# The hats of all fourteen columns formed by ScalarE in SBUF, and every engine's order drawn up anew

## The reference, cut to what matters

```python
out = relu(bn(conv1x1(x)))
offset = conv3x3(out)                      # 18 rows: (dy, dx) for each of 9 taps
py = y + k // 3 - 1 + dy;  px = x + k % 3 - 1 + dx
val = bilinear samples of out at (py, px), zero outside
out = relu(bn(conv1x1(bn(einsum("bckhw,ock->bohw", val, w)))))
```

## Time and profile before

| | us |
|---|---|
| median of 3 runs | 1134.95 |
| lowest and highest | 1133.67, 1144.43 |
| the profiled execution | 1137.99 |
| its span, first to last instruction | 1135.9 |
| busy in it: PE, DVE, ACT, POOL | 949.5, 766.0, 552.7, 355.2 |
| TensorE clock granted, mean share | 0.87 |
| moved by DMA | 123.31 MB |

### The profile page before, as it was taken

How to read it: one execution, slowest core, us unless ns; L and a number is a source line. 1 busy time by engine, 2 the same in 40 slices (tenths; PEclk the granted TensorE clock), 3 DMA queues, 4 the chain that set the end, 5 groups by cost and what they waited for, 6 DMA issues and landing times.

```text
span 1135.9 us, 19270 instructions
## 1 busy us (share of the span) xinstructions
PE 949.5 (84%) x7176; PEld 651.0 (57%) x7176; DVE 766.0 (67%) x2047; ACT 552.7 (49%) x1155; POOL 355.2 (31%) x320
## 2 busy tenths in 40 slices
PE   3779798998889898989889898989898998867534
PEld 2546476665656565756566665656575665545222
DVE  2658375868778795959596876968595958555232
ACT  1134353737365564647383736546464737261502
POOL 2012415243233414152433323250515233233100
PEclk9688769899999898989898996979898989886756
DMA  9011251424425161615243442516161524334160
GB/s 221 16 33 29 60 170 41 149 89 119 136 79 179 55 194 52 201 36 173 80 150 101 119 136 75 180 54 194 48 189 50 152 85 131 114 97 143 27 170 15
DMA packets 116546, 123.31 MB, mean 109 GB/s; under 512 B 64802, under 2 KB 99750, under 8 KB 116454
## 3 DMA queue, kind: packets, MB, share of 16 engines
q1 hardware_dynamic: 103492, 83.33, 26.0%
q10 hardware_dynamic: 6818, 25.04, 6.4%
q0 software_dynamic: 6144, 13.71, 4.0%
HBM read 84.32 MB, written 37.73 MB: 107 GB/s over the span
## 4 chain that ended last, share of the span: by engine, by line
PE 52%; DVE 15%; DMA 10%; issue 9%; ACT 6%; POOL 5%; SPq 1%; ACTq 1%; POOLq 0%; DVEq 0%
PE ps L620 49%; DMA y_turned<-b_yt 6%; POOL b_yp L1234 4%; DMA b_yp<-y_turned,b_to 4%; DVE x L1280 2%; ACT c_pad L955 2%; DVE y L1277 1%; PE ps L834 1%; DVE st L1307 1%; SPq L1795 1%; DVE b_adt L1272 1%; ACT y L955 1%; DVE b_yt L1283 1%; DVE y L1280 1%; PE ps L798 1%
## 5 line engine op out<-in xcount | busy, mean ns | idle before, releaser
L1234 POOL DMA_INDIRECT b_yp<-y_turned,b_to x64 | 82.5, 1289 | 311.0 <-DMA y_turned<-b_yt 296.4
L620 PE MATMUL ps<-y,inw 128*128 128x392 f32 x384 | 141.4, 506 | 0.2 <-DVE y L1277 0.2
L1186 POOL TENSOR_TENSOR rs<-ve,root 128x4 f32<-128x4 f32 x64 | 65.8, 1029 | 219.4 <-DVE ve L1276 219.0
L620 PE MATMUL ps<-c_w,c_zt 126*64 126x196 f32 x896 | 109.2, 400 | 21.5 <-DMA c_zt<-z_turned 18.0
L1307 DVE BATCH_NORM_STATS2 st<-x 128x6 f32<-128x196 f32 x256 | 73.5, 349 | 76.8 <-POOL x L1186 68.0
L620 PE MATMUL ps<-w,a_S 128*32 128x384 f32 (+2 forms) x1280 | 91.9, 431 | 26.2 <-DVE a_S L1280 24.1
L620 PEld LDWEIGHTS ps<-c_w,c_zt 126*64 126x64 f32 x896 | 73.7, 168 | 53.7 <-issue 36.4
L1272 DVE TENSOR_TENSOR c_w<-c_w,c_hat 126x1176 f32<-126x1176 f32 (+1 forms) x64 | 97.6, 1580 | 8.9 <-DMA c_w<-hat_turned 8.9
L955 ACT ACTIVATE x<-ps,cvec 128x392 f32<-128x392 f32 x32 | 18.7, 587 | 167.1 <-PE ps L620 167.1
L620 PEld LDWEIGHTS ps<-y,inw 128*128 128x128 f32 x384 | 69.3, 193 | 39.5 <-issue 3.0
L1208 POOL DMA_INDIRECT x_turned<-b_xt,b_to x64 | 63.6, 994 | 55.1 <-DVE b_xt L1283 43.1
(11 more groups left out here) (201 smaller groups left out, 2087.4 us busy)
## 6 DMA issues: line engine op xcount, KB each, us to landing
z_turned<-c_z SPq DMA_DIRECT2D x32, 441.0 KB
c_zt<-z_turned SPq DMA_DIRECT2D x16, 882.0 KB
c_w<-hat_turned ACTq DMA_DIRECT2D x16, 771.8 KB
c_w<-hat_turned SPq DMA_DIRECT2D x16, 771.8 KB
c_w<-hat_turned ACTq DMA_DIRECT2D x16, 578.8 KB
c_w<-hat_turned SPq DMA_DIRECT2D x16, 578.8 KB
b_xp<-x_turned SPq DMA_DIRECT2D x32, 222.0 KB
x<-in_x SPq DMA_DIRECT2D x32, 196.0 KB, 2.7
```

What stands on the lines that cost most here:

```text
L620: return nc.tensor.matmul(o, l, r, start=start, stop=stop)
L1186: return nc.gpsimd.tensor_tensor(out=o, in0=x, in1=y, op=op)
L1234: nc.gpsimd.indirect_dma_start(out=YP[:, m, h].rearrange("p b d -> p (b d)"), out_offset=None, in_=y_dram[g % 2], in_offset=bass.IndirectO ...
```

## The change

The constant `expand` gives, for the column part, the distance without the column: the sampled place px itself, the same on all 14 partitions of a tap. ACT keeps |py - vy| from f2.3 (Abs) and copies px beside it; f2.4 applies Relu to the row half alone. A new step f2.6 of ACT, four parts (two column pieces by two samples), forms the column hats in `c_w`: one Abs per column with bias -vx, 28 per group in all, and then one Relu with scale -1 and bias 1 over the piece. Its first part waits until PE has read the first six columns of the group before (`c_free`), its third until the accumulation before is finished. The stores and loads of hats go, with their semaphores and DRAM tensor, from SP and from ACT. DVE's product waits for `c_near` instead of the load. PE's instructions stay the same, but for the count after d2.2c. All of `PLAN` and `FROM` is new; `FROM` steps by 56793 per group, where it stepped by about 60897.

What follows from the new tables for a middle group (g), as the order in which parts stand:

- PE: n0(g), s1.1d to f(g-2), o1.0a(g-3), c0.8(g-1), o1.0b, k3.3(g-5), ta.0a(g-2), c0.10(g-1), o1.2a, b, ta.0b, c, c0.11, ta.0d, d2.2a, b(g-4), n2(g-3), c0.13(g-1), d2.2c to g(g-4), f2.1(g-3), d2.4(g-4), c0.1(g), n3(g-4), f2.2(g-3), c0.2(g), f2.3, f2.5a to d(g-3), n1(g-1), k3.1(g-4), f2.5e to h, c0.4(g), tb.7, 10, 11, 12(g-2), s1.1a, b(g-1), tb.20(g-2), c0.5(g), k3.2(g-4), tb.21a, b(g-2), s1.1c(g-1), c0.6(g).
- ACT: c0.1(g), f2.1(g-3), tb.0(g-2), k3.0(g-4), f2.3(g-3), tb.3(g-2), f2.4, f2.5a, b, k3.1, f2.5c, d, c0.4(g), tb.9, tb.10(g-2), **f2.6a, b(g-3)**, tb.20(g-2), s1.1a, b(g-1), tb.21(g-2), c0.5(g), **f2.6c**, k3.2(g-4), **f2.6d**, s1.1c, d(g-1), c0.7(g), s1.1e, f, s1.2, s1.4, c0.8(g), c0.10, k3.3a, ta.0a, k3.3b, o1.2(g-2), ...
- SP: x load of g, ta.3(g-3), tb.22(g-3), f2.6(g-4), d2.1(g-4), store of the result (g-6). Before, f2.5, f2.6, d2.0 and d2.1 of g-4 stood ahead of tb.22(g-3).

```diff
-            expand[at + 2, 1, k] = k % 3 - 1 - np.arange(HW)
+            expand[at + 2, 1, k] = k % 3 - 1
...
 # PE, d2.2
+                    if part == 2:
+                        last.then_inc(c_free.sem, 1)
...
 # ACT, f2.3
-                    fn(c_hat[b][:, :, :].rearrange("p x n -> p (x n)"), R.tile(("ex", b), g)[0:TV, 0:2 * N], ACT.Abs)\
-                        .then_inc(R.drained(("ex", b), g), 1)
+                    t = R.tile(("ex", b), g)
+                    fn(c_hat[b][:, 0, :], t[0:TV, 0:N], ACT.Abs)
+                    fn(c_hat[b][:, 1, :], t[0:TV, N:2 * N], ACT.Copy).then_inc(R.drained(("ex", b), g), 1)
 # ACT, f2.4
-                    x = c_hat[b][:, :, :]
+                    x = c_hat[b][:, 0, :]
                     fn(x, x, ACT.Relu, scale=-1.0, bias=1.0).then_inc(c_hat_ok.sem, 1)
...
+                if i == 6:
+                    h, b = part // G, part % G
+                    if part == 0:
+                        if first(g):
+                            act.wait_ge(ranked, 1)
+                        else:
+                            act.wait_ge(c_free.sem, c_free.count(g - 1))
+                    if part == G and g:
+                        filled(act, "acc", g - 1, H)
+                    drained(act, ("ex", b), g)
+                    cols = VSPLIT[h]
+                    for vx in range(cols.start, cols.stop):
+                        last = fn(c_w[b][:, vx, :], c_hat[b][:, 1, :], ACT.Abs, bias=-float(vx))
+                    last.then_inc(c_apart.sem, 1)
+                    act.wait_ge(c_apart.sem, c_apart.count(g, part + 1))
+                    x = c_w[b][:, cols, :]
+                    fn(x, x, ACT.Relu, scale=-1.0, bias=1.0).then_inc(c_near.sem, 1)
...
 # DVE, d2.1
-                    v.wait_ge(*hat_in[b][h].at(g))
+                    v.wait_ge(c_hat_ok.sem, c_hat_ok.count(g, b + 1))
+                    v.wait_ge(c_near.sem, c_near.count(g, part + 1))
...
 # SP, f2.5 gone
-                    sp.wait_ge(c_hat_ok.sem, c_hat_ok.count(g, b + 1))
-                    sp.dma_start(hat_dram[g % 2][b].rearrange("t (v n) -> (t v) n", v=HW), c_hat[b][:, 1, :])\
-                        .then_inc(hat_out[b].sem(g), 16)
 # SP and ACT, d2.0 gone
-                    load_hats(sp, 0, part, g)
-                    load_hats(act, 1, part, g)
```

More of the change, by code:

```diff
@@ L236 @@
-    "once": (84039,),
+    "n0": (0, 56793, 113586, 170379, 227172, 283965, 340758, 397551, 454344, 511137, 567930, 624723, 681516,
+        738309, 795102, 851895),
+    "c0": (0, 56793, 113586, 170379, 227172, 283965, 340758, 397551, 454344, 511137, 567930, 624723, 681516,
+        738309, 795102, 851895),
+    "n1": (0, 56793, 113586, 170379, 227172, 283965, 340758, 397551, 454344, 511137, 567930, 624723, 681516,
+        738309, 795102, 851895),
+    "s1": (0, 56793, 113586, 170379, 227172, 283965, 340758, 397551, 454344, 511137, 567930, 624723, 681516,
+        738309, 795102, 851895),
@@ L237 @@
+    "once": (0,),
 }
@@ L250 @@
-        (297390,),
-        (300106, 300746, 302963),
-        (61968, 106689, 119060),
+        (8985,),
+        (52229, 56876, 59874, 62685, 63959, 64065, 66772, 70906, 80609, 93597),
+        (115294,),
+        (118326, 118806, 120447, 122707, 122707, 122931),
+        (125505, 128858, 133753, 137402),
+        (175000, 175000, 175000, 175000, 175000, 175000, 175000, 175709, 177066, 177066),
+        (179724, 180523, 184493, 185293),
+        (201722,),
+        (211260, 226189, 228832, 228832, 228832, 228832, 228832, 229220, 229456, 229456, 229834),
@@ L253 @@
+        (250989, 256881, 263977, 265303, 265588, 266448, 266448, 270176),
+        (281812,),
+        (285916, 290610, 294110),
+        (64065, 67667, 102457),
     ),
     "vector": (
[L255 to L260, removed]
@@ new lines @@
+        (88148, 95706),
+        (102906, 115992, 122547, 125928),
+        (132258, 134277, 145401),
+        (145401, 152283, 152495, 152495, 152495, 153570, 154420, 159699, 159699, 160584, 160584, 160584, 160584,
+        162774, 165677, 165677, 165677, 171572),
+        (182845, 186630),
+        (189584, 191394, 196270),
+        (202362, 209076, 209076, 210622, 211214),
+        (226587, 226587, 234567, 239468, 257797, 257877),
+        (257877, 258468, 258779),
+        (301783, 312375),
@@ L304 @@
         (),
-        (725433, 726423),
-        (745848, 745848),
-        (),
-        (),
-        (793133, 793133, 794662, 794662),
-        (795338, 799009, 801675),
-        (),
-        (966006,),
-        (545804, 576221),
+        (461002, 462247),
+        (472862, 472862),
+        (),
+        (),
+        (537059, 537935),
+        (537935,),
+        (),
+        (657912,),
+        (266502, 275592),
     ),
@@ L582, in build @@
         z_in = landed("z_in")
-        hat_out = [landed(f"hat_out{b}") for b in range(G)]
-        hat_in = [[landed(f"hat_in{b}_{h}") for h in range(2)] for b in range(G)]
+        c_apart = sig("distances", 2 * G)
+        c_near = sig("hats_along_row", 2 * G)
+        c_free = sig("c_w_read")
         c_w_ok = sig("c_w", 2 * G)
@@ L600, in drained @@
             eng.wait_ge(ring.drained(f, g), ring.done(f, g))
[L602 to L609, removed]
-            lo, hi = VSPLIT[h].start * N, VSPLIT[h].stop * N
-            eng.dma_start(c_w[b][:, VSPLIT[h], :].rearrange("p v n -> p (v n)"),
-                          hat_dram[g % 2][b][:, lo:hi].unsqueeze(1).to_broadcast([TAPS, HW, hi - lo]))\
-                .then_inc(hat_in[b][h].sem(g), 16)
         block = ctx.enter_context(nc.Block())
```

134 lines of the change are left out of this document (51 added, 83 removed), and 6 rows, old and new, of the table PARTS.

## The result

The changed kernel takes 1183.5 us (median of 4, 1180.31 to 1185.31) against 1137.99 us for the kernel before (median of 4, 1133.67 to 1144.43): a ratio of 1.039, 95% interval 1.033 to 1.045. It is slower by 4%, where 1130 us was forecast with a range up to 1176. The profiled execution took 1183.74 us.

What follows compares the result with a forecast made beforehand. TensorE bounds the kernel, through an order in which it also waits. Steps +5, filling +4, draining -11 on 1137.99 us gave 1136, then 1133 at the median, shaded to 1130 us; range 1082 to 1176.

Steps and rivals of the forecast that it cites:

- The queue of SyncE: Sync queue issuing y_turned earlier: up to 3 us off the gather path; stall of 2.40 us falls to 0.5 (0 to 2.5).
- covered by some 5 us: Sync queue: c_zt sets out later, but its store and load land before d2.2a with some 5 us to spare.
- PE's own work does not change: TensorE in the new order: its own work stays as before, so the step changes only by stalls, +0.3 us.
- rival C: ACT becomes the pacer between Exp and b_us: step of 63.8 us, 1168 us; chance 0.27, clock included.
- The hats: Hats on ACT: 28 Abs, 7.8 us, and four Relus, 5.4 us, add 13.2 us per pair of samples.
- `c_pad`'s 2.6 us: TensorE, new order: c_pad must wait for c0.1, leaving PE 2.6 us idle per step, against 1.40 before.
- The ring: Seven PSUM tiles: the sixth z product waits for a tile ACT copies after Ln, some 0.7 us (0 to 1).
- `c_off`, 1.4: TensorE waits for c_off behind other DVE work: 1.4 us per step, against 0.48 before.
- Filling: Start of the kernel: the first pair's last transposes stand behind the second pair's work, +4 us (0 to +6).
- draining: End of the kernel: without the hats' loads ahead of c_zt it is shorter, taken as -11 us.
- Rival B: The new order closes PE's gaps: step of 59 us, 1092 us; chance 0.28.
- the summed stalls, 6.2 us: TensorE's stalls per step after the change: 6.7 us summed, say 6.2 allowing for overlap, against 5.9 before.

Runs made afterwards that it cites:

- e10: Changed kernel, z_turned store and order kept, with the c_zt load (and the result's stores behind it) waiting until the y gather has landed: 1089.18 us, ratio 0.961.
- e12: Changed kernel with the z_turned store moved ahead of y_turned and the c_zt load made to wait for y_turned's landing: 1108.82 us, ratio 0.978.
- e3: Changed kernel without the four Relus of a group on c_w (that part of the computation left out): 1169.41 us, ratio 1.027.
- e9: Changed kernel with the z_turned store moved ahead of y_turned and without the four Relus on c_w: 1079.28 us, ratio 0.954.
- e7: Changed kernel with the z_turned store, behind y_turned on the sync queue, waiting until the y gather has landed: 1160.38 us, ratio 1.018.
- e2: Functions of the kernel before (hats through DRAM) in the changed kernel's order, with the z_turned store ahead of y_turned: 1120.31 us, ratio 0.981.
- e6: Kernel before with an extra unread store of z_turned's size (2 x 441 KB) right behind the y_turned store: 1151.58 us, ratio 1.006.
- e11: Kernel before with an extra unread 882 KB copy, the size of c_zt, started when y_turned has landed: 1173.72 us, ratio 1.038.
- e5: Changed kernel's functions (hats on ACT) in the order of the kernel before, some later parts moved to follow the hats: 1148.92 us, ratio 1.012.

## Why the prediction was wrong

**The step that failed** is in "The queue of SyncE": "up to 3 us come off this path, and the stall of 2.40 us goes ... 0.5 us stays (0 to 2.5)". It measured 0.52 + 4.59 = 5.1 us in the step shown, 77.6 us in all. Two products use the gathers. In the kernel before either of them waits: in the step of the earlier trace rows the second, 2.40 us, in the step of the earlier trace rows the first:

```profile
366.17 0.59 PE L834 MATMUL ps<-c,b_yp 98*128 98x98 f32 x4 [1.32 <-DMA b_yp<-y_turned,b_to]
```

For the first product the forecast came true: from the copy of `b_yt` to it 8.8 us (10.7 in that step before), with 0.52 us of wait, as forecast. The second is the one that failed. I had seen that `z_turned` and `c_zt` now go out behind `y_turned`, and priced this only as lateness of `c_zt`, "covered by some 5 us". That was right: PE never waits for it. I did not ask beside what they, and the result's stores behind them, would run. The path to the second product grew: from the copy of `b_yt` (431.75) to the second product it is 16.1 us, against 13.3 before; in e10 it is 475.64 - 463.08 = 12.6. The removed 47 MB of hats quietened the DMA engines everywhere but in the 4 to 5 us that decided.

**The second is "PE's own work does not change."** In instructions it doesn't; in time a step of the windows has 3.1 us more of it. I named the clock as an aid to rival C, with 1 to 2 us, and looked for it in another place. The trace shows it right behind the stall, and e10 shows that it goes with the stall. The Trainium skill, page "TensorE: Matmul & The Clock Gate" (HAM oscillation — how this bites in real kernels), tells of the same pattern, a wait for a DMA after which PE runs cold. The rows agree: 0.50 granted behind the wait of 4.59 us in the changed kernel, 0.52 behind that of 2.28 us in e12.

**The hats.** 13.2 us a step forecast; (121.4 + 48.3 + 37.9) / 16 = 13.0 measured, by these groups of ACT:

```profile
L945 ACT ACTIVATE c_w<-c_hat 126x196 f32<-126x196 f32 x448 | 121.4, 362 | 0.0
...
L945 ACT ACTIVATE c_w<-c_w 126x1568 f32<-126x1568 f32 x32 | 48.3, 1511 | 1.0
L945 ACT ACTIVATE c_w<-c_w 126x1176 f32<-126x1176 f32 x32 | 37.9, 1184 | 1.0
```

Rival C, ACT as the pacer, gave a time nearest to the result (1168), but by the wrong cause, so its nearness is luck: its sign, PE idle for ACT's `b_us`, is not among PE's waits at all, and e3 and e9 put ACT's share for the Relus at 12 to 14 us or less.

**The other stalls.** `c_pad`'s 2.6 us: an idle time of 2.18 us is there in most steps, but what ends it is DVE's statistics for n3 (39.5 us in all), whose product stands ahead of `c_pad`'s. I had named `c_pad`, and the row for it has 2.9 us once. Later in the step shown, that product starts at 471.62 and `c_pad` is done at 472.25, so `c_pad` would have held PE about as long. The ring, 0.7: 9.5 us in 13 waits, 0.7. `c_off`, 1.4: 4.9 us in three waits, so mostly covered. Filling +4 measured +5.1; draining -11 measured -9.1, with no wait for `c_zt`.

**Rival B** (a step of 59 us, 1092) is what this order gives once the load and the result's stores are out of the way: e10 has a step of (1000.88 - 108.55) / 15 = 59.5 us and 1089 us. Its chance of 0.28 was not wrong about the order; the summed stalls, 6.2 us, were 8.3 in the changed kernel and 59.6 - 53.9 = 5.7 in e10.

## What to carry over

When transfers change places in a queue, it is not enough to ask whether each still arrives in time: draw the 5 us around the transfer that the critical path waits for, and list what else the DMA engines will do in them, and what releases each of those transfers. A stall of 4 us ahead of TensorE can cost as much again in clock (39.0 us of waiting and 55.1 us of busy time between the changed kernel and e10). A wait put on a bulk load, so that it starts behind the urgent gather, cost nothing that these runs show and was worth 8% (1183.5 to 1089.2 us). e7 shows the limit: with the store held back too, the load itself came late.

## What was not expected of the hardware

- A load of 882 KB with 392 KB of stores behind it, together at up to 366 GB/s, delayed a gather issued 2.2 us behind the load: its product starts 5.3 us after the end of its issue and waits 4.59 us, where without them it waits 1.08 us; a store of as many bytes, at 200 GB/s beside the first gather, left its product with a wait of 0.52 and 0.48 us (changed kernel and e10).
- After one wait of 4.59 us the next 9 us of matmuls were granted 0.50 to 0.53 of full speed; after one of 2.28 us (e12) it was 0.52, and full again 4 us later; after one of 1.08 us (e10) it stayed full. In the kernel before, a wait of 1.32 us was followed by 0.57 (366.20 to 368.70). So the length of the last wait alone does not tell what is granted behind it.
- Still open: POOL's own time to issue a gather, 1289 ns on average before and 1269 in e2 (1330 in e6, 1309 in e11), is 1534 to 1587 in the new order with hats on ACT, 1408 and 1429 without the Relus, and 1114 in e5. Which neighbour lengthens it wasn't tried.
